# A decoder block in 8 tiles: spread set-up, split scores, a bias row in the up-projection, other orders

## The reference, cut to what matters

```python
x = x + attn(layernorm(x))      # A: rotating state, causal convolution, gated delta rule over 16 heads
x = x + xattn(layernorm(x), ctx, ctx)   # C: 2*16 heads against 64 context rows, softmax(q k) v, difference of two maps
x = x + ffn(layernorm(x))       # D: convolution, 8 experts (top 2), then the feed-forward end
# in A:   q, k = l2norm(q), l2norm(k)
# in C:   scores = q*SCALE @ k ; p = softmax(scores) ; p @ v
# in D:   ff = gelu(h @ ff_down_w.T + ff_down_b) ; return h + ff @ ff_up_w.T + ff_up_b
```

## Time and profile before

| | |
|---|---|
| median of 3 runs | 1863.15 us (1862.46 to 1866.17) |
| the profiled execution's own time | 1863.28 us |
| its span (first to last instruction) | 1861.5 us |
| PE busy, share of the span | 87% |
| DVE busy | 70% |
| ACT busy | 45% |
| POOL busy | 12% |
| granted TensorE clock, mean share of full | 0.955 |

### The profile page before, as it was taken

One profiled execution on the slowest core, in us unless ns is written; L12 is line 12 of the kernel. 1 busy time (PEld: TensorE's weight loads), 2 busy tenths in 40 slices (PEclk: granted clock), 3 DMA queues, 4 the chain that ended last, 5 costly groups with the idle time before them and its releaser, 6 DMA issues.

```text
span 1861.5 us, 42720 instructions
## 1 busy us (share of the span) xinstructions
PE 1628.5 (87%) x17048; PEld 1091.6 (59%) x17048; DVE 1294.8 (70%) x3152; ACT 844.0 (45%) x1513; POOL 216.9 (12%) x204
## 2 busy tenths in 40 slices
PE   1676999998999899899999899998999989998777
PEld 1354675566665666566655666566755666655654
DVE  7366668866688667876589576876688666884642
ACT  1172247533474346633384345642475434743422
POOL 0031001210031001210021100310012100310000
PEclk8785899999999999999999999999999999999889
DMA  4010000100010000100010000100001000100000
GB/s 177 23 35 3 12 1 15 22 14 13 1 35 2 25 1 12 24 3 24 1 35 2 14 12 12 24 3 25 1 12 24 10 6 1 35 2 13 1 1 12
DMA packets 19832, 32.05 MB, mean 17 GB/s; under 512 B 1305, under 2 KB 17713, under 8 KB 19505
## 3 DMA queue, kind: packets, MB, share of 16 engines
q1 hardware_dynamic: 19634, 29.22, 5.5%
HBM read 20.81 MB, written 8.39 MB: 16 GB/s over the span
## 4 chain that ended last, share of the span: by engine, by line
PE 67%; DVE 13%; issue 9%; ACT 7%; POOL 2%; DMA 0%; DVEq 0%; POOLq 0%; ACTq 0%; SPq 0%
PE bank L1668 11%; PE four L1403 6%; PE bank L1629 5%; PE bank L1317 4%; PE bank L1617 3%; PE bank L1344 3%; PE four L1405 3%; PE bank L1607 3%; PE four L1344 3%; PE four L1490 3%; POOL kq L482 2%; PE four L1539 2%; PE bank L1323 2%; PE four L1523 2%; PE bank L1337 2%
## 5 line engine op out<-in xcount | busy, mean ns | idle before, releaser
L1668 PE MATMUL bank<-w_sb,cs 128*128 128x512 f32 x512 | 264.8, 620 | 0.0
L775 ACT ACTIVATE cs<-bank 128x512 f32<-128x512 f32 x128 | 75.1, 592 | 164.2 <-PE bank L1323 164.0
L1277 DVE SCALAR_TENSOR_TENSOR cs<-cs,rwt 128x256 f32<-128x256 f32 x224 | 125.8, 562 | 22.8 <-ACT cs L775 17.3
L732 ACT COPY cs<-bank 128x512 f32<-128x512 f32 x128 | 74.8, 584 | 135.3 <-PE bank L1617 135.3
L676 ACT ACTIVATE qkv<-mk,c_sb 128x256 f32<-128x256 f32 x256 | 108.7, 497 | 58.0 <-PE four L1490 55.5
L1629 PE MATMUL bank<-vx_sb,cs 128*128 128x136 f32 x1024 | 131.8, 282 | 0.0
L1344 PE MATMUL bank<-c_sb 128*128 128x128 f32 x912 | 126.2, 287 | 5.6 <-issue 5.6
L1344 PEld LDWEIGHTS bank<-c_sb 128*128 128x128 f32 x912 | 115.8, 199 | 20.5 <-issue 17.8
L1668 PEld LDWEIGHTS bank<-w_sb,cs 128*128 128x128 f32 x512 | 88.6, 194 | 65.7 <-issue 60.4
L1629 PEld LDWEIGHTS bank<-vx_sb,cs 128*128 128x128 f32 x1024 | 125.7, 191 | 0.0
L1403 PE MATMUL four<-hT,w_sb 128*128 128x512 f32 x256 | 121.6, 597 | 2.2 <-DVE rotb L956 2.2
(11 more groups left out here) (246 smaller groups left out, 3284.0 us busy)
## 6 DMA issues: line engine op xcount, KB each, us to landing
w_sb<-in_weights SPq DMA_DIRECT2D x1, 5752.0 KB, 20.3
xt<-in_x SPq DMA_DIRECT2D x8, 512.0 KB, 3.8
hT<-in_x SPq DMA_DIRECT2D x8, 512.0 KB, 3.8
vscr<-qkv SPq DMA_DIRECT2D x8, 512.0 KB, 3.9
vT<-vscr SPq DMA_DIRECT2D x32, 128.0 KB, 4.4
out<-cs SPq DMA_DIRECT2D x8, 512.0 KB, 3.1
qkv<-in_scratch SPq DMA_DIRECT2D x1, 528.0 KB, 4.9
hT<-in_scratch SPq DMA_DIRECT2D x2, 256.0 KB, 5.7
```

The lines of the kernel that those rows point to most:

```text
L732: fin("pt_sb", nc.scalar.copy(flat(probT[:, 4 * n:4 * n + 4, :]), bank[6][:, :]))
L775: fin("moe_act", A(ye[:, u % 4, :], bank[4 + (u + 1) % 4][:, :], ACT.Silu))
L1277: ins = stt(comb[:, b, :], src, wgt, comb[:, b, :], ALU.mult, ALU.add)
L1668: mm(dst, x1T[:, k, b * TB:b * TB + TB], ew[:, k, ep * 512:ep * 512 + 512], start=k == 0, stop=False)
```

## The change

Set-up. `x`'s first tile is loaded third, weights come in three pieces with a semaphore each, in the order of use, and the context's pieces go to the space of the second half (`stage`, the slots of `cs`). The bias row is laid over 28 partitions (102 numbers each). DVE starts with the memsets, which wait for nothing. The first layer norm and its copy are taken out of the first tile (`head`) and stand between pieces of the set-up. The reciprocal becomes ln and exp on ACT. What only the second half needs becomes steps that stand in the first tile at the places of steps of `SECOND` (`prologue`): key and value projections on PE at `turn4` and `pw`, their copies on ACT there, on DVE the weight scaling at `dconv` and the spreading of keys and values at `acc.0` to `acc.9`.

```diff
-            sp.dma_start(w_sb[:, :], weights[:, :]).then_inc(ld_w, 16)
-            sp.wait_ge(su["ready"], 1)
+            sp.dma_start(xt[:, :, :], x[:, 0:TB, :].rearrange("b p d -> p b d")).then_inc(x_in.sem, 16)
+            load_weights(["cin"], ld_cin)
+            load_scratch(ramp, "ramp", ld_ramp)
+            sp.dma_start(bias_row, biases[:, :]).then_inc(ld_b, 16)
+            load_weights(["dw", "ctrl"], ld_proj)
+            for n, name in enumerate(("wk", "wv", "ctx")):
+                load_scratch(stage[:, 512 * n:512 * n + 512], name, ld_ctx)
+            load_scratch(stage[:, 2048:3072], "ctxd", ld_ctx)
+            load_weights(["wo", "ffu"], ld_rest)
...
-            take(first(0), None)
+            take(head or first(0), prologue)
...
+            # DVE, after the memsets, the angle's reduction and the copy into kq
+            head = first(0)
+            head.pop("ln1")()
+            dve.wait_ge(su["trig"], 1)
+            do(V.tensor_copy(sinT[:, 0:1], small[:, 16:17]))
+            do(V.tensor_copy(cosT[:, 0:1], small[:, 17:18]))
+            for _ in range(3):
+                double()
+            ramp_one()
+            head.pop("turn1")()
+            split_bias()
+            while trig[0] < TB:
+                double()
+            do(ts(sinT[:, :], sinT[:, :], C("sgn"), None, ALU.mult))
+            dve.wait_ge(su["ramp"], 1)
+            dve.wait_ge(ld_proj, 16)
+            do(stt(dw, dw, L("condnorm"), ramp, ALU.mult, ALU.mult))
+            turns(dve, "dve", first, second, head, {"dconv": scale_weights, "acc": context})
...
+            # ACT
+            head = first(0)
+            head.pop("ln1")()
+            act.wait_ge(ld_ramp, 16)
+            A(ramp, ramp, ACT.Exp, scale=-1.0).then_inc(su["ramp_exp"], 1)
+            act.wait_ge(su["lam_in"], 1)
+            A(small[:, 20:22], small[:, 22:24], ACT.Exp).then_inc(su["lam"], 1)
+            head.pop("turn1")()
+            act.wait_ge(su["ramp_one"], 1)
+            A(ramp, ramp, ACT.Ln).then_inc(aset, 1)
+            act.wait_ge(aset, 1)
+            A(ramp, ramp, ACT.Exp, scale=-1.0).then_inc(su["ramp"], 1)
+            turns(act, "act", first, second, head, {"turn4": k_copy, "pw": v_copy})
...
+            turns(pe, "pe", first, second, None, {"turn4": k_proj, "pw": v_proj})
```

Scores, bank by bank. `sc.u` becomes `sc.u.0` and `sc.u.1`, each both f of one group a, with a semaphore of its own; `max` waits for each bank and frees each:

```diff
-                def sc(u):
-                    b, hc = u // 2, u % 2
-                    up("psub", u) if u else up("qx_sb")
+                def sc(u, a):
+                    b, r = u // 2, 64 * (u % 2) + 32 * a
+                    up("psub", 2 * u - 1 + a) if u else up("qx_sb")
                     for f in range(2):
-                        for a in range(2):
-                            r = 64 * hc + 32 * a
-                            last = mm(bank[4 + a][:, 256 * f:256 * f + 256], qx[r:r + 32, f, b * TB:b * TB + TB], kbx[r:r + 32, f, b, :], start=True, stop=True)
+                        last = mm(bank[4 + a][:, 256 * f:256 * f + 256], qx[r:r + 32, f, b * TB:b * TB + TB], kbx[r:r + 32, f, b, :], start=True, stop=True)
                     fin("sc_ps", last)
```

Up-projection. The bias is row 65 of the weights and row 65 of `gT` is ones; rows 66 to 128 of both are zero. The product has 128 rows, and the bias product goes:

```diff
-        gT = cs[0:HID, 7, 0:T]
+        gT = cs[:, 7, T:2 * T]
...
-                        mm(dst, gT[:, b * TB:b * TB + TB], ffu, start=True, stop=False)
-                        last = bias(dst, "up")
+                        last = mm(dst, gT[:, b * TB:b * TB + TB], ffu, start=True, stop=True)
```

Norms. The multiplications of `norm`, and the addition of `x1T`, are written with the three-operand instruction and the constant 1.0:

```diff
-                        fin("qk_norm", tt(kqf[:, j, :, 1, :], v3(qkv[:, j, :]), tmp, ALU.mult))
+                        fin("qk_norm", stt(kqf[:, j, :, 1, :], v3(qkv[:, j, :]), 1.0, tmp, ALU.mult, ALU.mult))
```

```diff
-KEEP = {("turn1",): 9, ("rot",): 1, ("unrot",): 1, ("raw", 0): 1, ("tinv", 0): 1, ("tinv", 1): 1, ("tinv", 2): 2,
-        ("tinv", 4): 1, ("tinv", 6): 4, ("tinv", 7): 4, ("wo",): 9, ("turn2",): 8, ("qx",): 5, ("pt", 14): 3,
-        ("wp",): 3, ("turn4",): 2, ("pw",): 6, ("router",): 10, ("moe", 2): 1, ("mo",): 3, ("turn6",): 11, ("ffd",): 2,
-        ("ffu",): 3, ("db",): 2, ("sum", 0): 1, ("sum", 1): 6}
+KEEP = {("turn1",): 9, ("unrot",): 1, ("raw", 0): 4, ("tinv", 1): 4, ("tinv", 3): 1, ("tinv", 5): 1, ("onorm",): 2,
+        ("wo",): 11, ("turn2",): 12, ("pv", 6): 2, ("turn3",): 1, ("wp",): 2, ("pw",): 7, ("router",): 6,
+        ("turn5",): 3, ("mo",): 1, ("turn6",): 12, ("ffu",): 6, ("proj", 0): 7, ("db",): 1}
```

More of the change, by code:

```diff
@@ L310, in flat @@
             return t3.rearrange("p a b -> p (a b)")
[L312 to L316, removed]
+        stage = flat(cs)
+        wk_, wv_, ctx_ = [stage[:, 512 * n:512 * n + 512].rearrange("p (k n) -> p k n", k=KC) for n in range(3)]
+        k_sb = stage[:, 1536:2048]
+        ctxd_ = stage[:, 2048:3072].rearrange("p (k b n) -> p k b n", k=KC, b=B)
+        ramp = stage[:, 3072:4128]
+        v_sb = stage[:, 5120:6144].rearrange("p (n v) -> p n v", v=DH)
+        bias_row, bias_rest = [stage[0:NBR, 6144 + 128 * n:6144 + 128 * n + NBIAS // NBR] for n in range(2)]
+        bias_part = [stage[0:NBR, 6400 + 64 * n:6400 + 64 * n + NBIAS // NBR // 2].bitcast(BF16) for n in range(3)]
         RAW = (2, 3, 0, 1)
@@ L349, in build, with turns @@
         block = ctx.enter_context(nc.Block())
-        def turns(eng, engine, first, second):
+        def turns(eng, engine, first, second, head=None, prologue=None):
             def take(*halves):
@@ L514, in _ @@
             A(small[:, 16:18], small[:, 18:20], ACT.Sin).then_inc(su["trig"], 1)
[L516 to L522, removed]
-                nc.scalar.copy(kn[:, 1, h2 * 256:h2 * 256 + 256], bank[h2][:, 0:256])
-            act.wait_ge(su["vproj"], 1)
-            for n in range(2):
-                nc.scalar.copy(flat(M3[:, 32 * n:32 * n + 32, :]), bank[2 + n][:, :]).then_inc(su["kv_sb"], 1)
             def inv_sqrt(ch, dst, src, eps, scale, done):
@@ L796, in ffd_ @@
                     up("ffd_ps")
-                    fin("gelu", A(gT, bank[6][0:HID, :], ACT.Gelu, bias=L("fdb")[0:HID, :]))
+                    fin("gelu", A(gT[0:HID, :], bank[6][0:HID, :], ACT.Gelu, bias=L("fdb")[0:HID, :]))
                     if isinstance(j, int):
@@ L802, in second, with k_copy, v_copy @@
                         "pw": pw_, "top": top, "moe": moe, "turn5": turn5, "hnorm": hnorm, "turn6": turn6, "ffd": ffd_}
-            turns(act, "act", first, second)
+            def k_copy():
+                act.wait_ge(su["k_ps"], 1)
+                for n in range(2):
+                    last = nc.scalar.copy(k_sb[:, 256 * n:256 * n + 256], bank[4 + n][:, 0:256])
+                last.then_inc(su["k_sb"], 1)
+            def v_copy():
+                act.wait_ge(su["v_ps"], 1)
+                for n in range(2):
+                    last = nc.scalar.copy(flat(v_sb[:, 32 * n:32 * n + 32, :]), bank[6 + n][:, :])
+                last.then_inc(su["v_sb"], 1)
+            head = first(0)
[10 more added lines that the diff above has]
+            turns(act, "act", first, second, head, {"turn4": k_copy, "pw": v_copy})
         @block.vector
@@ L878, in _, with split_bias @@
-            for h2 in range(2):
-                for b in range(B):
+                trig[0] = 2 * n
+            def split_bias():
+                dve.wait_ge(ld_b, 16)
+                hi, mid, lo = bias_part
+                do(V.tensor_copy(hi, bias_row))
+                do(tt(bias_rest, bias_row, hi, ALU.subtract))
+                do(V.tensor_copy(mid, bias_rest))
+                do(tt(bias_rest, bias_rest, mid, ALU.subtract))
+                do(V.tensor_copy(lo, bias_rest))
+                V.nop().then_inc(su["split"], 1)
@@ new lines, in ramp_one, with scale_weights @@
+            def ramp_one():
+                dve.wait_ge(su["ramp_exp"], 1)
+                ts(ramp, ramp, 1e19, 1.0, ALU.min, ALU.add).then_inc(su["ramp_one"], 1)
+            def scale_weights():
+                dve.wait_ge(su["lam"], 1)
+                do(tt(turns_, small[:, 20:21], small[:, 21:22], ALU.subtract))
+                do(ts(nlam, turns_, -1.0, -LAMBDA_INIT, ALU.mult, ALU.add))
+                dve.wait_ge(ld_rest, 16)
+                ts(W("wo"), W("wo"), L("outnorm"), None, ALU.mult)
+                do(ts(W("wp"), W("wp"), L("subln"), 1.0 - LAMBDA_INIT, ALU.mult, ALU.mult))
@@ L1238, in x1T_ @@
                     for k in range(KC):
[L1239 removed]
+                        last = stt(r3(x1T[:, k, :]), r3(sT[:, k, :]), 1.0, fT[:, k, :, 2:TB + 2], ALU.mult, ALU.add)
                     fin("x1T", last)
@@ L1719, in second @@
                         "turn5": turn5, "mo": mo, "turn6": turn6, "ffd": ffd_, "ffu": ffu_}
-            turns(pe, "pe", first, second)
+            turns(pe, "pe", first, second, None, {"turn4": k_proj, "pw": v_proj})
 def layout(v):
```

166 lines of the change are left out of this document (79 added, 87 removed).

## The result

| | before | after |
|---|---|---|
| median of the runs timed together (4 each) | 1864.2 us | 1799.4 us (1797.1 to 1801.2) |
| profiled execution, its span | 1861.5 | 1798.4 |
| end of the first tile's last addition | 209.9 | 175.9 |
| a turn, mean of 7 (from one such addition to the next) | 213.9 | 209.5 |
| tail, from the last one to the end | 154.0 | 155.7 |

The ratio is 0.965 (95% interval 0.9635 to 0.9668): 65 us faster, where 45.6 were forecast. Of the difference between the spans, 63.1 us, set-up and first tile give 34.0, the seven turns 30.8, and the tail takes back 1.7.

The account below looks back on a forecast made before the run. PE was taken to bound the turns, DVE the set-up. From 1863.3 us, set-up and first tile -33.4, seven turns -11, tail -1.6 and +0.4 for its scores, together -45.6, gave 1817.7, rounded 1818; range 1792 to 1842.

Parts of the forecast that it names:

- Set-up: Time up to the first rotation, bound by DVE: rotation starts at 29.1 instead of 68.61, -39.5 us, between -42 and -33.
- The covers named: In set-up, loads, ACT's ln and exp, and PE's first product at either clock were to stay hidden behind DVE's list.
- Its rival: Set-up gains little: a load or DVE's list holds the rotation to 37 instead of 29; 1826 us, chance 0.08.
- The return in the first tile: Work moved out of set-up onto PE, ACT and DVE in the first tile: +6.1 us, between +2 and +12.
- Scores: 64 score steps on PE, bank by bank: halves still overlap, +0.05 us each, +3 in all, bounds -8 and +53.
- the rival's 0.83: Score halves don't overlap on PE: 0.83 us more for each of 64 steps, +53 instead of +3.2; 1868 us, chance 0.08.
- Norms: Three-operand norm products on DVE wait for POOL as well: 0, bounded by +0.4 and -2.2 us for a turn.
- Up-projection: PE saves 1.64 us for each tile: -1.2 us counted for a turn (bounds 0 and -1.6), -1.6 in the tail.
- The new tables: Seven fills less, 1.6 us of PE, half arriving: -0.8 us a turn; new places' waits taken as 0, bounds +3 and -5.
- the tables shorten it by 3 more: Rival in the turns: idle PE and fills could become work, a turn 3 us shorter still; 1797 us, chance 0.15.
- The tail: Time after the last turn: -1.6 us from the up-projection and +0.4 for its scores.

Follow-up runs that it names:

- s1: Kernel after with scores joined, separate bias product, two-operand norms and the old tables, so only the spread set-up is left: 1840.3 us, ratio 0.9881.
- s3: Kernel after with the old tables (places and fills), each second score half right behind the first: 1839.0 us, ratio 0.9870.
- s7: Kernel after with scores joined, two-operand norms and the old tables; spread set-up and new up-projection are left: 1839.5 us, ratio 0.9868.
- s9: Kernel after with the second group of each score step reading the same 32 partitions as the first (wrong scores): 1859.3 us, ratio 0.9981.
- s5: Kernel after with the old places on all three engines, new fills kept: 1859.9 us, ratio 0.9975.
- s4: Kernel after with the old fills (their steps and counts), new places kept: 1813.4 us, ratio 0.9751.
- s8: Kernel after with five fills ahead of the query projection again: 1792.5 us, ratio 0.9616.
- s11: s8 with more fills in PE's waits in the tail alone: 1782.0 us, ratio 0.9571.
- s10: s8 with fills in the first tile alone: 40 ahead of the first `z`, 3 ahead of each other, 1 in each half `co`: 1802.8 us, ratio 0.9660.

## Why the prediction was right, and where its sum was not

- **Set-up: right.** Rotation at 28.94, forecast 29.1. The covers named (loads, ACT's ln and exp, PE's product at either clock) held. Its rival is dead.
- **The return in the first tile: right as a sum.** Set-up and first tile -34.0, forecast -33.4. `k_proj` takes the 1.7 us that were counted, and DVE's solve with four pieces of `kbx` in it takes 1.45 longer (13.92 for 12.47), where 1.8 were counted. But s1 and s3 show that 5 to 6 us of the stage are owed to the new tables, which the sum took for nothing here; alone, the set-up is worth 22 us with the old ones. That the stage's sum came out within 0.6 is in part luck. The sum took the stages' clock as given.
- **Scores: right.** Last pass of a step at 0.765 us against 0.758, a price near 0. s3 and s7, which differ by the split of the scores and the form of the norms alone, show no price either (ratios 0.9870 and 0.9868). s9 measures the rival's 0.83 as 0.85; that kernel took 1859.3, the rival's 1868 had started from a forecast 18.6 too high. The sentence of the Trainium skill on which that rival rested, that matmuls stay in program order, holds in s9, where both groups lie in the same rows of the array. In the kernel after it doesn't: a pass of the second group starts 0.013 us behind the first pass of the first group, ahead of three that stand in front of it in the program. The measurement decides. The same page (TensorE: Matmul & The Clock Gate, section "Part 3: Packing small matmuls — row/col tiling") says that products in different row groups run concurrently; these runs agree, and it is this section that bears on the case.
- **Norms: right.** 2.85 us in both forms, 0 in time.
- **Up-projection: the mechanism right, its size a bit low.** 1.54 us of PE for each tile (forecast 1.64). PE's lateness at `wo` is gone. 16 us in all with the new tables where -1.2 and -1.6 (10 in all) were counted. That little of it is left with the old tables, s7, no term of the forecast knew.
- **The new tables: the step that failed.** "What the new places do to the waits no row shows. I bound it by +3 and -5 for a turn ... and take 0." The tables are worth 5.2 us for a turn and 40 in all, where 0.8 was counted for a turn and nothing for the first tile. For a turn that is inside the bound (0.8 and 5), but s5 shows that the two don't add up: the new places alone are worth 3.5 us for a turn with the old fills and 8.0 with the new. Counted from the measured 213.9 (the one turn that the forecast read lasted 215.0), the forecast was a turn of 212.3 where 209.5 was measured. Over seven turns 30.8 us came where 11 were counted; these 19.8, with 0.6 more in the first tile and 2.9 back in the tail, make the 17.5 between the forecast's 45.6 and the spans' 63.1. The rival "the tables shorten it by 3 more", 1797, is the case that came, given 0.15. A small slip beside it: of the fills, 11 fewer stand between the start of the attention and the router and 4 more elsewhere, not 13 and 6; the 7 in all is right.
  What the step overlooked is two things. The larger is the order itself: with no low stretch that costs, the new places save 2.2 us of a turn, by the waits ahead of `z`, and the new fills 1.1 (210.3 in s7's first turn, 208.1 in s4's, 207.0 after). The smaller, the 1.9 that are left of the 5.2, is by subtraction the clock: in the timeline of the turn of the earlier trace rows the down-projection ran at half clock, and the fills were read as work to be saved. Places and fills decide on which instruction PE's low stretches lie, and with that whether 1.6 us of PE arrive or not. s5, s7 and s8 show it from three sides: fewer fills made it slower, less work made it hardly faster, more fills made it faster.
- **The tail: wrong in sign.** +1.7 instead of -1.2. The up-projection's four sequences did take 1.6 less, but `qx` ran at half clock (6.61 us instead of 3.60, and the scores start 1.3 later), and ahead of `ffu` stand 12 fill passes for 6, partly at half clock, 2.42 us for 0.94. s8 takes 1.3 us of this back, and s11 shows what all the tail's low stretches cost, 12.

What stays open: why the low stretch of a turn lies on the experts' products in one turn and on `qx` or `raw` in the next, with the same instructions. It may move between executions of one kernel too, which would explain why they lie up to 11 us apart (s10: 1793.6 to 1805.0) and why the mean clock differs between them (0.955 to 0.962 after); with one trace for each kernel this isn't shown.

## What to carry to other kernels

Where PE bounds a loop and its clock falls now and then, list the low stretches of each turn and what PE does in them, before pricing any edit: one ahead of a long enough wait is free, one in the chain costs up to half its length (1.5 to 1.7 us for one of 3.4 here, 1.9 for one of 6.8 on `raw`). Work taken from PE just ahead of a wait can come back as a low clock behind it, so try fills in that wait before the gain is called lost (s7 itself was not run with them); a fill belongs in a wait longer than itself, never in a chain. And order tables are to be tested as a whole: here either half of the new ones, put into the old, misled.

## What was unexpected of the hardware

Fills in waits of the tail held the clock at 1.00 for 141 us and made a stage whose other engines did the same work 12.0 us shorter (154.4 to 142.4), with 174 passes more. In the recurrence of the first tile 77 fills, 154 passes, didn't (0.50 over the last 40.9 us of it) and cost 10. Passes in other rows of the array start ahead of passes that stand before them in the program (1673.330 against 1673.637). And 0.56 us more of waiting ahead of the transposes (2.07 to 2.63) went with 1.6 us more in what followed.
